# Attention with single float32 products in place of three fp32r products of split operands

## What is computed

```python
x1 = _ln(x) * (1.0 + scale1) + shift1
qkv = (x1 @ qkv_w + qkv_b).reshape(Bc, Tc, 3, H, DH)
q, k, v = (qkv[:, :, 0], qkv[:, :, 1], qkv[:, :, 2])
attn = jnp.einsum('bthd,bshd->bhts', q, k) * scale
attn = jax.nn.softmax(attn, axis=-1)
attn_out = jnp.einsum('bhts,bshd->bthd', attn, v).reshape(Bc, Tc, INNER)
attn_out = attn_out @ out_w + out_b
x = x + gate1 * attn_out
...
h = jax.nn.gelu(x2 @ ffn_w1 + ffn_b1, approximate=False)
x = x + gate2 * (h @ ffn_w2 + ffn_b2)
...
w1 = _ternary_weight(W_fc, GROUP)
h = jnp.einsum('bsd,hd->bsh', x, w1)
h = jnp.square(jax.nn.relu(h))
hn = _rms_norm(h)
w2 = _ternary_weight(W_proj, GROUP)
return jnp.einsum('bsh,dh->bsd', hn, w2)
```

## Time and profile before

| | |
|---|---|
| time of three runs | 392.17, 392.4 and 393.11 us; median 392.4 us |
| span of the profiled execution, first to last instruction | 391.2 us |
| TensorE matmuls, weight loads | 367.8 us (94%), 319.5 us (82%) |
| VectorE, ScalarE, GpSimd | 288.0 us (74%), 237.0 us (61%), 129.7 us (33%) |
| mean granted TensorE clock | 0.980 of full speed |

### The profile page before, as it was taken

How to read it: one execution, slowest core, us unless ns; L and a number is a source line. 1 busy time by engine, 2 the same in 40 slices (tenths; PEclk the granted TensorE clock), 3 DMA queues, 4 the chain that set the end, 5 groups by cost and what they waited for, 6 DMA issues and landing times. The chain is left out here.

```text
span 391.2 us, 6260 instructions
## 1 busy us (share of the span) xinstructions
PE 367.8 (94%) x2096; PEld 319.5 (82%) x2096; DVE 288.0 (74%) x486; ACT 237.0 (61%) x582; POOL 129.7 (33%) x111
## 2 busy tenths in 40 slices
PE   2899999999999999999999999999889899996975
PEld 2789888888888888888888898889778787885855
DVE  5775569768776976866887667689988638797793
ACT  1464576665666566656676566775687358573751
POOL 1522224321542232272323144335423300162451
PEclk9999999999999999999999999999999999998995
DMA  7913031000303100030200012010000000000002
GB/s 231 358 61 108 1 109 54 2 0 3 108 0 107 54 0 0 0 107 29 78 0 0 0 26 83 0 55 1 2 0 1 2 0 2 0 1 2 8 19 80
DMA packets 11778, 16.53 MB, mean 42 GB/s; under 512 B 672, under 2 KB 7920, under 8 KB 11760
## 3 DMA queue, kind: packets, MB, share of 16 engines
q1 hardware_dynamic: 11760, 16.30, 12.6%
HBM read 15.25 MB, written 1.05 MB: 42 GB/s over the span
## 5 line engine op out<-in xcount | busy, mean ns | idle before, releaser
L345 POOL TENSOR_TENSOR prob<-prob,rinv 128x512 f32<-128x512 f32 x32 | 33.4, 1043 | 152.4 <-DVE rinv L788 152.4
L980 PE MATMUL bank<-x_hi,wqk_hi 128*128 128x512 f32 x128 | 54.4, 425 | 0.0
L982 PE MATMUL bank<-x_hi,wqk_lo 128*128 128x512 f32 x128 | 51.3, 401 | 0.0
L981 PE MATMUL bank<-x_lo,wqk_hi 128*128 128x512 f32 x128 | 51.1, 399 | 0.0
L706 DVE TENSOR_TENSOR v_lo<-bank,v_hi 128x512 fp32r<-128x512 f32 x30 | 20.7, 691 | 39.2 <-ACT v_hi L427 39.2
L493 ACT ACTIVATE prob<-bank,nbias 128x128 f32<-128x128 f32 x128 | 45.1, 370 | 4.1 <-DVE nbias L782 4.1
L427 ACT ACTIVATE p_split<-bank 128x512 fp32r<-128x512 f32 x32 | 19.1, 598 | 35.4 <-PE bank L1014 35.4
L461 ACT ACTIVATE o_hi<-pv_pair,bias 128x512 fp32r<-128x512 f32 x31 | 21.3, 688 | 24.3 <-PE pv_pair L1029 24.3
L982 PE MATMUL bank<-k_hi,q_lo 128*128 128x128 f32 x128 | 35.4, 276 | 0.0
L417 POOL TENSOR_TENSOR raw_qk<-raw_qk 128x512 f32<-128x512 f32 x13 | 18.4, 1415 | 50.7 <-ACT raw_qk L622 50.4
L981 PE MATMUL bank<-k_lo,q_hi 128*128 128x128 f32 x128 | 35.2, 275 | 0.0
(11 more groups left out here) (206 smaller groups left out, 1086.9 us busy)
## 6 DMA issues: line engine op xcount, KB each, us to landing
raw_qk<-in_L_cond_qkv_w_dram SPq DMA_DIRECT2D x8, 512.0 KB, 4.9
raw_v<-in_L_cond_qkv_w_dram SPq DMA_DIRECT2D x4, 512.0 KB, 3.8
raw_o<-in_L_cond_out_w_dram SPq DMA_DIRECT2D x4, 512.0 KB, 3.6
xt<-in_x_dram SPq DMA_DIRECT2D x2, 512.0 KB, 5.0
xr<-in_L_cond_ada_w_dram SPq DMA_DIRECT2D x1, 1024.0 KB, 10.2
raw_w<-in_L_cond_ffn_w_dram SPq DMA_DIRECT2D x2, 512.0 KB, 7.6
t_raw<-in_L_ffn_W_fc_dram SPq DMA_DIRECT2D x4, 256.0 KB, 3.8
t_raw<-in_L_ffn_W_proj_dram SPq DMA_DIRECT2D x4, 256.0 KB, 3.9
```

The source lines that it names most:

```text
L345: nc.gpsimd.tensor_tensor(e, e, rinv[:, j % 2, :].unsqueeze(2).broadcast_to([P, SQ, P]), ALU.mult).then_inc(norm_done, 1)
L980: nc.tensor.matmul(dst, ah, bh, start=start and n == 0, stop=False)
L981: nc.tensor.matmul(dst, ah, bl, start=False, stop=False)
L982: m = nc.tensor.matmul(dst, al, bh, start=False, stop=stop and n == len(terms) - 1)
```

## The change

Queries, keys, probabilities and values are kept in one piece (`qT`, `kT`, `probT`, `vals`). Scores, value products and sums of squares are single matmuls of plain float32 operands. All other products stay split.

- `scores`: four matmuls in place of twelve. They wait for `q_done` and `k_done`.
- `pv`: four matmuls of 128 columns into one bank (`BO`) in place of four of 256 and four of 128 into `pv_pair`.
- `sum_squares`: four matmuls in place of eight, straight from `h2_sum`.
- ScalarE copies the queries with their bias (`keep_q`) and the values (`keep_v`). VectorE copies the keys with their bias (`keep_k`) and the probabilities (`keep_p`). The other halves' steps are gone: `k_hi`, `q_lo`, `v_lo`, the `hi` half of the probabilities, `sum_hi` and `sum_lo`.
- The attention output is still split, since it enters `out_product`; `o_lo_part` is now one step, straight from one bank.
- The hidden values of the FFN have buffers `hid_hi` and `hid_lo`; `vals` lies at the same address as `hid_hi`. The output of the last unit but one goes to `o2_hi` and `o2_lo`.

```diff
+        hid_at = nc.sbuf_base
+        hid_hi = sb("hid_hi", [P, NC, TQ], F32R)
+        hid_lo = sb("hid_lo", [P, NC, TQ], F32R)
+        vals = nc.alloc_sbuf_tensor_at("vals", [P, B, HG * P], F32, offset=hid_at)
+        qT = sb("qT", [P, TQ])
+        kT = sb("kT", [P, TQ])
...
+        probT = sb("probT", [P, SQ, P])
...
-            def p_hi_part(i):
-                act.wait_ge(t_mm, i + 1)
-                hi_part(p_split[:, :, 0, :], bank[BV][:, :].rearrange("p (s t) -> p s t", s=SQ), p_h)
...
+                nc.scalar.activation(vals[:, b, :], bank[src][:, :], ACT.Copy).then_inc(v_done, 1)
+
+            def keep_q(G, j):
+                biased_hi(qT[:, :], bank[BQ][:, :], HG * G + QB + j % HG, q_mm, UG * G + j + 1, q_done)
...
-                    biased_hi(q_hi[:, :], bank[BQ][:, :], HG * G1 + QB + j1 % HG, q_mm, i + 2, q_h)
-                    biased_hi(k_hi[:, :], bank[BK][:, :], HG * G1 + KB + j1 % HG, k_mm, i + 2, k_h)
+                    keep_q(G1, j1)
...
-            def sum_hi(quad):
-                act.wait_ge(sq_sum, (NC - 1) * (quad + 1))
-                hi_part(h2_hi[quad][:, :], h2_sum[:, quad, :], sum_h)
...
+            def keep_p(i):
+                dve.wait_ge(t_mm, i + 1)
+                nc.vector.tensor_copy(probT[:, :, :].rearrange("p s t -> p (s t)"), bank[BV][:, :]).then_inc(p_done, 1)
+
+            def keep_k(G, j):
+                dve.wait_ge(k_mm, UG * G + j + 1)
+                nc.vector.tensor_scalar(kT[:, :], bank[BK][:, :], bias[:, bass.ds(HG * G + KB + j % HG, 1)], None, ALU.add).then_inc(k_done, 1)
+
+            def o_lo_part(G, j):
+                hi, lo = head_output(UG * G + j)
+                dve.wait_ge(o_h, UG * G + j + 1)
+                nc.vector.scalar_tensor_tensor(out=lo[:, :], in0=bank[BO][:, :], scalar=bias[:, bass.ds(HG * G + VB + j % HG, 1)],
+                                               in1=hi[:, :].bitcast(F32), op0=ALU.add, op1=ALU.subtract).then_inc(o_l, 1)
...
             def scores(i, first):
-                pe.wait_ge(k_l, i + 1)
+                pe.wait_ge(q_done, i + 1)
+                pe.wait_ge(k_done, i + 1)
...
-                    m = split_mm(bank[BS][:, t], [(q_hi[:, t], q_lo[:, t], k_hi[:, t], k_lo[:, t])])
+                    m = nc.tensor.matmul(bank[BS][:, t], qT[:, t], kT[:, t], start=True, stop=True)
...
-                    nc.tensor.matmul(pv_pair[:, at:at + 2 * P], v_hi[:, b, h], p_split[:, s, :, :].rearrange("p x t -> p (x t)"),
-                                     start=True, stop=False)
-                    m = nc.tensor.matmul(pv_pair[:, at:at + P], v_lo[:, b, h], p_split[:, s, 0, :], start=False, stop=True)
+                    m = nc.tensor.matmul(bank[BO][:, s * P:(s + 1) * P], vals[:, b, h], probT[:, s, :], start=True, stop=True)
...
-                pe.wait_ge(sum_l, quad + 1)
+                pe.wait_ge(sq_sum, (NC - 1) * (quad + 1))
                 for s in range(SQ):
-                    for n, part in enumerate((h2_hi[quad], h2_lo[quad])):
-                        m = nc.tensor.matmul(bank[(BY, 0)[quad]][:, 2 * s:2 * s + 2], part[:, s * P:(s + 1) * P], ones[:, :],
-                                             start=n == 0, stop=n == 1)
+                    m = nc.tensor.matmul(bank[(BY, 0)[quad]][:, 2 * s:2 * s + 2], h2_sum[:, quad, s * P:(s + 1) * P], ones[:, :],
+                                         start=True, stop=True)
```

More of the change, by code:

```diff
@@ L89, in adaln_block @@
         w2_lo = sb("w2_lo", [P, NC * D], F32R)
[L91 to L96, removed]
+        hid_at = nc.sbuf_base
[4 more added lines that the diff above has]
+        kT = sb("kT", [P, TQ])
+        o2_hi = sb("o2_hi", [P, TQ], F32R)
+        o2_lo = sb("o2_lo", [P, TQ], F32R)
         prob = sb("prob", [P, 2, SQ, P])
-        p_split = sb("p_split", [P, SQ, 2, P], F32R)
+        probT = sb("probT", [P, SQ, P])
         o_hi = sb("o_hi", [P, TQ], F32R)
@@ L128, in adaln_block @@
         scratch = sb("scratch", [P, SQ])
-        ones = sb("ones", [P, 2], F32R)
+        ones = sb("ones", [P, 2])
         ms = sb("ms", [P, B])
@@ L143, in adaln_block @@
         h2_sum = raw_qk[:, 2:4, :]
-        h2_hi, h2_lo = (q_hi, k_hi), (q_lo, k_lo)
         w1_chunks, wv_chunks, wo_chunks = (
@@ L151, in adaln_block @@
         w2T = wqk_lo[:, :, :].rearrange("p a b -> p (a b)")
[L152 to L159, removed]
+        bank = [ctx.enter_context(nc.psum_tensor(f"bank{n}", [P, TQ], F32)) for n in range(8)]
         cond_in, arow_in, bias_in, ada1_in, ada2_in = (
@@ L180, in adaln_block @@
             sem(n) for n in ("q_mm", "k_mm", "s_mm", "t_mm", "v_mm", "pv_mm", "out_mm"))
[L181 to L184, removed]
+        q_done, k_done, exp_done, p_done, v_done, o_h, o_l = (
+            sem(n) for n in ("q_done", "k_done", "exp_done", "p_done", "v_done", "o_h", "o_l"))
+        max_done, nb_done, rinv_done, y_acc = (sem(n) for n in ("max_done", "nb_done", "rinv_done", "y_acc"))
         norm_done = sem("norm_done")
@@ L241, in head_output @@
         def head_output(i):
-            return (q_hi, q_lo) if isinstance(i, int) and i == NU - 2 else (o_hi, o_lo)
+            return (o2_hi, o2_lo) if isinstance(i, int) and i == NU - 2 else (o_hi, o_lo)
         def hidden(quad, c):
             if quad == 1:
-                return v_hi[:, c, :], v_lo[:, c, :]
+                return hid_hi[:, c, :], hid_lo[:, c, :]
             if c < 4:
@@ L539, in unit @@
                     o_hi_part(*before(G, j))
-                if last and j == UG - 1:
-                    p_hi_part(i)
                 if vs:
-                    v_hi_part(vs[1], v_count(G, j, 1), BQ)
+                    keep_v(vs[1], v_count(G, j, 1), BQ)
             act.wait_ge(small_t, 1)
@@ L556, in _ @@
             act.wait_ge(small_cp, 3)
-            biased_hi(q_hi[:, :], bank[BQ][:, :], QB, q_mm, 1, q_h)
-            biased_hi(k_hi[:, :], bank[BK][:, :], KB, k_mm, 1, k_h)
+            keep_q(0, 0)
             modulate(1, SHIFT1, SCALE1, bank[6:8])
-            v_hi_part(0, 1)
+            keep_v(0, 1)
             wqk_hi_part(2, 32)
@@ L790, in unit @@
                     G1, j1 = (G, j + 1) if j < UG - 1 else (G + 1, 0)
-                    biased_lo(q_lo, bank[BQ], HG * G1 + QB + j1 % HG, q_hi, q_h, i + 2, q_l)
+                    keep_k(G1, j1)
                     if last and j == UG - 2:
                         add_residual(0)
-                    biased_lo(k_lo, bank[BK], HG * G1 + KB + j1 % HG, k_hi, k_h, i + 2, k_l)
-                if vs:
-                    v_lo_part(vs[0], v_count(G, j, 0))
                 if j == 5:
@@ L830, in _ @@
             dve.wait_ge(small_cp, 3)
-            biased_lo(q_lo, bank[BQ], QB, q_hi, q_h, 1, q_l)
-            biased_lo(k_lo, bank[BK], KB, k_hi, k_h, 1, k_l)
+            keep_k(0, 0)
             modulate(1, SHIFT1, SCALE1, bank[6:8])
-            v_lo_part(0, 1)
             unit(0, 0, (), True)
-            v_lo_part(1, 2, V_FIRST[1])
-            for b in range(2, SQ):
-                v_lo_part(b, b + 1, V_FIRST[b])
             ada_part(1, GATE1, NA, SCALE2, bank[7])
@@ L1080, in unit @@
                 if vs:
-                    pe.wait_ge(q_l, i + 2)
+                    pe.wait_ge(q_done, i + 2)
                     v_block(VG, vs[1], BQ)
```

74 lines of the change are left out of this document (22 added, 52 removed).

## The result

The changed kernel takes 374.74 us (median of four runs, 374.35 to 375.05), the kernel before beside it 392.69 us. The ratio is 0.957 (95% interval 0.954 to 0.960): 18 us less, where 13.4 were forecast. The time lies inside the range of 374 to 383 us, 0.7 us from its lower end. The profiled span is 373.2 us against 391.2.

What follows compares the result with a forecast made beforehand. In attention TensorE's queue, with scores paced by weight loads, was taken to bound the kernel. Scores 12.8 us, end of attention 0.6 us and other terms 0 gave 13.4 us off: 379.0 us, range 374 to 383 us.

Steps and rivals of the forecast that it cites:

- What bounds it: In attention TensorE's queue sets the pace, and a score matmul is paced by its weight load, about 0.11 us, not its columns.
- The first rival: Score and value products: a record's two streams are not hidden beside its weight load, 0.218 us a record; 432 us, chance 7%.
- the second (streams, 406 us): Score and value products: TensorE's streams bind, not its loads, each product costing 0.053 us more; 406 us, chance 2%.
- Scores, 12.8 us: Scores in attention: eight records at 0.1175 us replace twelve, saving 0.40 us in each of 32 units; bounds 14.4 and 12.2 us.
- This buys 0 directly: VectorE and ScalarE steps removed in each attention unit gain 0 directly where TensorE is never idle.
- The fourth rival: In each unit, scores, maximum, exponentials, reciprocal, keys or transposes end last, making 0.4 us a wait; 391 us at worst, chance 4%.
- Value products 0: Value products in attention: eight records before and after, gain 0; bounds 1.3 us gained and 1.0 us lost over 32 units.
- Sum of squares 0: Sum of squares: eight float32 records replace eight fp32r ones, both paced by loads, and the removed splits gain 0.
- End of attention 0.6 us: End of attention: one-step `o_lo` shortens TensorE's second wait, and later steps inherit most of it; 0.6 us gained, or 0.
- The clock: Rival on half-clock falls: three more take 5 us, 384 us; without the one at 37 us, 377 us; three or more, chance 5%.
- from the FFN on: FFN and ternary stage: same instructions in other buffers, gain 0.

## Why the prediction was right, and where not

- **What bounds it: right.** TensorE's queue sets the unit, and narrow float32 records keep the pace of the narrow fp32r ones, which is that of their weight loads. The first rival (loads not overlapped, 432 us) and the second (streams, 406 us) fell with the first row of scores. The second had the number of streams right, four a product at 512 columns; its price was wrong, since at 128 columns they add nothing to the 0.11 us of a record.
- **Scores, 12.8 us: mechanism right, size low.** The term took 0.1175 us a record, from the pace of 256 columns and of the mixed value product. It is 0.112 us (0.90 / 8), next to the lower bound of 0.111 that it named. That makes 0.44 us a unit instead of 0.40, and the units gained 0.448: 14.3 us over 32.
- **"This buys 0 directly" for VectorE and ScalarE: the step that failed.** The forecast looked for the cover that had to hold when the unit gets shorter, and checked keys (0.4 us to spare) and probabilities (2.1 us). The fourth rival's list of chains lacks this one, too. The forecast saw that a bank with a value block comes free one pass earlier, called it a wait that only gets shorter, and gave it no price. That chain had 0.02 us to spare. With it left in place 14 units give back 0.40 us each (5.6 us of the 18), shown from both sides: put back into the changed kernel +5.9 us, taken out of the kernel with single scores -4.2 us. That the sum held is luck in this point: the 12.8 us needed that pass gone, the change happens to remove it, and the forecast did not know that it mattered. By the text's own terms single scores alone would have been 12.8 us, and were 8.3.
- **Value products 0: right.** 0.88 us against 0.87.
- **Sum of squares 0: right within the noise,** 0.2 to 0.3 us in the trace.
- **End of attention 0.6 us: right in size,** 0.78 us up to the first FFN product. Without the 0.45 us of the scores, TensorE comes to the first projection 0.96 us earlier, to the second 1.12, and to the first FFN product 0.78. As forecast, steps in front of the FFN take part of the gain back, here through the waits for `probT` and `x_lo`. The second `o_hi` starts 0.38 us earlier by the same count, so ScalarE's queue did hold it, though not quite as firmly as forecast.
- **The clock: not in the sum.** The forecast had a profile without the fall at 377 us; the trace bears out 1.6 us for its 1.7. That this execution had no fall and the one before it had one is, by the spans above, probably chance. In that case it is a part of the 18 us that the change cannot claim.

The miss in numbers: 17.9 - 13.4 = 4.5 us, of which 1.5 in scores (14.3 - 12.8), 0.2 at the end of attention, 1.6 by the clock, and 1.2 at the program's start (0.5) and from the FFN on (0.7), which the forecast had at 0. No run explains the 1.2, and single executions differ as much: the kernel before, profiled again, reached unit 2 0.7 us sooner. The measured time lies inside the range by 0.7 us, less than the clock's part. With such a fall it would have been about 376 us (an estimate, 374.74 + 1.6), nearer to the forecast of 379.0.

## What to carry to other kernels

Price a product of plain float32 operands by both limits, its weight loads and its streams, at its own width: here one float32 product beats three fp32r ones at 128 columns (0.22 against 0.33 us) and loses at 512 (0.86 against 0.68 us). When a stage on the critical engine gets shorter, list every chain that runs beside it, from the release of each PSUM bank too, with its spare time; a chain with 0.02 us to spare showed no idle time and no wait in this profile. And two parts of a change can each be worth little alone and much together, so test a part by taking it out as well as by doing it alone. Last, 2 us between two profiles can be one fall of the clock: look at the spans of all runs before giving such a difference to the change.

## What the runs showed of the hardware that was not expected

- A float32 record of 128 columns costs the same 0.111 us as an fp32r record of 128 columns, though at 512 columns it takes nearly twice the time (0.428 against 0.228 us). A product is two records: 0.22, 0.43 and 0.86 us at 128, 256 and 512 columns.
- TensorE's clock was halved for 3.4 us in the middle of a stretch in which it was never idle in the profile, in both profiles of the kernel before and in none of the ten others. The spans of the other runs suggest that this changes from execution to execution.
